# Writing the attention mask of every second token tile into PSUM with ScalarE instead of two products on TensorE

## The reference

```
qkv = x @ Wqkv;  q, k, v = split(qkv)            # 16 heads of 64
q = rope(l2norm(q) * qs);  k = rope(l2norm(k) * ksc)
sim = einsum('bhwie,bhwje->bhwij', q, look(k)) * 8      # 32 queries x 64 keys a window
mask = (it < jb) | (it > jb + w) | (jb == -1)
sim = where(mask, -big, sim);  attn = softmax(sim)
out = einsum('bhwij,bhwje->bhwie', attn, look(v)) @ Wo
x = out + x
x = (a * gelu(gate)) @ W2 + b2 + x                # a, gate from layernorm(x) @ W1
```

## Time and profile before

| what | value |
|---|---|
| median of 3 runs | 4778.22 us |
| lowest and highest | 4775.92 and 4784.65 us |
| the profiled execution's own time | 4772.76 us |
| span of the profile | 4771.0 us |
| mean granted clock of PE | 0.958 |
| transformer stage in the span | about 200 to 3600 us |
| busy over the span | PE 91%, DVE 66%, ACT 57%, POOL 55% |

### The profile page before, as it was taken

One profiled execution on the slowest core, in us unless ns is written; L12 is line 12 of the kernel. 1 busy time (PEld: TensorE's weight loads), 2 busy tenths in 40 slices (PEclk: granted clock), 3 DMA queues, 4 the chain that ended last, 5 costly groups with the idle time before them and its releaser, 6 DMA issues. The chain is left out here.

```text
span 4771.0 us, 155839 instructions
## 1 busy us (share of the span) xinstructions
PE 4331.5 (91%) x69192; PEld 2789.7 (58%) x69192; DVE 3143.9 (66%) x4110; ACT 2702.9 (57%) x3930; POOL 2624.7 (55%) x1468
## 2 busy tenths in 40 slices
PE   7489999999999999999999999999974999788878
PEld 5256666666666666666666666666652554344435
DVE  3467776767677766777776766777733443599975
ACT  4246666656666666566656665666642343577743
POOL 0266666666666666666666666666632222477752
PEclk8689999999999999999999999999986999799989
DMA  2111112211222112211122122222111000211100
GB/s 56 52 33 42 47 45 63 49 47 43 51 57 52 44 44 57 55 46 42 48 65 50 41 48 54 54 49 48 43 34 33 1 1 1 89 75 72 72 35 16
DMA packets 230429, 221.10 MB, mean 46 GB/s; under 512 B 137656, under 2 KB 185793, under 8 KB 227713
## 3 DMA queue, kind: packets, MB, share of 16 engines
q1 hardware_dynamic: 229761, 211.13, 16.9%
HBM read 68.50 MB, written 4.03 MB: 15 GB/s over the span
## 5 line engine op out<-in xcount | busy, mean ns | idle before, releaser
L1018 POOL TENSOR_TENSOR tf_qk<-tf_qk,tf_rot 128x1024 f32<-128x1024 f32 x384 | 908.3, 2365 | 1099.5 <-DVE tf_rot L1392 1099.5
L1025 POOL TENSOR_TENSOR tf_qk<-tf_qk,tf_rn 128x1024 f32<-128x1024 f32 x384 | 722.3, 1902 | 126.2 <-ACT tf_rn L1273 125.5
L1084 PE MATMUL tf_psum<-tf_Wqkv,tf_xsT 128*128 128x512 f32 x1536 | 737.6, 603 | 41.5 <-issue 20.6
L1266 ACT ACTIVATE tf_sq<-tf_psum 128x1024 f32<-128x1024 f32 x384 | 393.1, 1024 | 502.8 <-DVE tf_rot L1392 502.8
L1388 DVE TENSOR_TENSOR tf_qk<-tf_psum,tf_table 128x1024 f32<-128x1024 f32 x384 | 467.4, 1217 | 219.4 <-PE tf_psum L1084 218.4
L1398 DVE TENSOR_REDUCE tf_ss<-tf_sq 128x16 f32<-128x1024 f32 x384 | 457.6, 1192 | 23.5 <-ACT tf_sq L1266 23.5
L1392 DVE TENSOR_TENSOR tf_rot<-tf_psum,tf_table 128x1024 f32<-128x1024 f32 x384 | 466.2, 1214 | 0.0
L1084 PEld LDWEIGHTS tf_psum<-tf_Wqkv,tf_xsT 128*128 128x128 f32 x1536 | 271.2, 192 | 320.6 <-issue 294.1
L1066 PE MATMUL tf_psum<-ident,tf_qk 128*128 128x128 f32 x3072 | 416.4, 279 | 7.3 <-issue 4.9
L1149 PE MATMUL tf_psum<-tf_probT,tf_Vback 64*64 64x32 f32 x12288 | 383.3, 221 | 29.8 <-DVE tf_z L1433 15.6
L1066 PEld LDWEIGHTS tf_psum<-ident,tf_qk 128*128 128x128 f32 x3072 | 349.1, 143 | 95.4 <-issue 87.5
(11 more groups left out here) (319 smaller groups left out, 7960.9 us busy)
## 6 DMA issues: line engine op xcount, KB each, us to landing
tf_Vback<-tf_V SPq DMA_DIRECT2D x384, 128.0 KB
tf_Vback<-tf_V SPq DMA_DIRECT2D x576, 64.0 KB
mb_Csb<-mb_kept SPq DMA_DIRECT2D x16, 2048.0 KB, 7.1
tf_zr<-z SPq DMA_DIRECT2D x96, 128.0 KB, 2.7
z<-tf_z SPq DMA_DIRECT2D x48, 256.0 KB, 2.5
tf_Wqkv<-in_Wqkv_split SPq DMA_DIRECT2D x18, 512.0 KB, 3.7
tf_zu<-z SPq DMA_DIRECT2D x97, 64.0 KB
tf_zu<-z SPq DMA_DIRECT2D x97, 63.5 KB
```

Of the source, the lines that this page charges most:

```text
L1018: nc.gpsimd.tensor_tensor(v, v, rot[:, kind, :], ALU.add).then_inc(added.sem, 1)
L1025: nc.gpsimd.tensor_tensor(v, v, rn[:, t, HEADS * kind:HEADS * (kind + 1)].unsqueeze(2) .to_broadcast([P, HEADS, HD]), ALU.mult).then_inc(n ...
L1084: last = nc.tensor.matmul(proj[:, half, :], xsT[:, step.unit(0), WIN + t * P:WIN + (t + 1) * P], Wqkv[:, c:c + 512], start=True, stop=True)
L1266: nc.scalar.activation(sq[:, kind, :], flat2(proj), ACT.Square).then_inc(squared.sem, 1)
```

## The change

For odd tiles (the second of a unit, `t` = 1) the two mask products are left out, and PE waits for a new event `opened` instead of `v_kept`. ACT writes the mask: `open_scores`, one ACTIVATE with the function Copy from the f32 mask in SBUF (`mask32`, the same 64 columns repeated for 16 heads) into both `score` banks, 128x1024. It stands in ACT's queue right behind `keep_v` in every even step (for the tile whose scores follow in the next, odd step), and waits for `keep_v` by its own semaphore `v_kept`. Even tiles keep their two products. No DMA and no other engine's instruction is changed.

```diff
@@ scores(step) on PE
                 pe.wait_ge(copied, place(step.before(), "k") + 2)
-                pe.wait_ge(v_kept.sem, v_kept.at(tau - 1, 1))
-                for odd in range(2):
-                    nc.tensor.matmul(score[:, odd, :], identb[:, :], mask[:, t:t + 1, :].to_broadcast([P, PAIRS, HD]),
-                                     start=True, stop=False, skip_group_check=True)
+                if t:
+                    pe.wait_ge(opened.sem, opened.at(tau // 2, 1))
+                else:
+                    pe.wait_ge(v_kept.sem, v_kept.at(tau - 1, 1))
+                    for odd in range(2):
+                        nc.tensor.matmul(score[:, odd, :], identb[:, :], mask[:, t:t + 1, :].to_broadcast([P, PAIRS, HD]),
+                                         start=True, stop=False, skip_group_check=True)
@@ on ACT
+            def open_scores(step):
+
+                act.wait_ge(v_kept.sem, v_kept.at(step.tile(2), 1))
+                nc.scalar.activation(score.rearrange("p b (a e) -> p (b a) e", e=HD),
+                                     mask32[:, 1:2, :].to_broadcast([P, HEADS, HD]), ACT.Copy).then_inc(opened.sem, 1)
@@ body(step) on ACT
                 if step.has(2):
                     keep_v(step)
+                    if step.k % 2 == 0:
+                        open_scores(step)
                 if step.has_input():
```

More of the change, by code:

```diff
@@ L844, in transformer_stage @@
         v_done, v_kept, pv_done, laid = ev("v_done"), ev("v_kept"), ev("pv_done"), [ev("laid0", 64), ev("laid1", 96)]
-        scored, maxed, centred, exped, den_sum, den_inv, prob_ready, o_copied, out_done, z_added = (
-            ev(n) for n in "scored maxed centred exped den_sum den_inv prob_ready o_copied out_done z_added".split())
+        scored, opened, maxed, centred, exped, den_sum, den_inv, prob_ready, o_copied, out_done, z_added = (
+            ev(n) for n in "scored opened maxed centred exped den_sum den_inv prob_ready o_copied out_done z_added".split())
         ln_stats, ln_moments, ln_logged, ln_rstd, xn_centred, xn_ready = (
@@ L1253, in _ @@
         def _(act):
-            for e in (squared, logged, rn_ready, v_kept, exped, o_copied, ln_logged, ln_rstd, gelued):
+            for e in (squared, logged, rn_ready, v_kept, opened, exped, o_copied, ln_logged, ln_rstd, gelued):
                 e.start(act)
```

## The result

The changed kernel takes 4842.73 us (median of 4 runs, 4839.4 to 4862.6) against 4779.9 us for the kernel before in the same session: a ratio of 1.0143, 95% interval 1.0124 to 1.0162. By the medians that is slower by 63 us, by the ratio by 68 (59 to 77), where the sum said 46. Measured again in a later session it was 1.0151 (1.0135 to 1.0167).

The account below looks back on a forecast made before the run. It took an ACT and DVE path to bound about 15 of some 66 us, PE the other 51. Terms +49.2, -4.7 and +1.5 at the edges gave +46.0, so 4824 us, likeliest range 4815 to 4833, 8 in 10 4798 to 4848.

Parts of the forecast that it names:

- The path over ACT and DVE without slack in step 3: From the kT copy in step 2 to `attend` in step 3: 15.12 us without slack, bounding the kernel there.
- the slot of 0.52 us on PE: PE's time for an odd tile's mask products before its scores; 96 x 0.52 = 49.9 us removed from PE's queue.
- step 2 to step 3: 46 places where the new ACT operation delays `gelu 1` and `attend` by 1.07 us, PE's saving lost: +49.2 us.
- step 0 to step 1: 47 places where scores wait for ACT's mask, so only 0.10 of the 0.52 us is won: -4.7 us.
- the argument against the clock: Each new wait is under 1 us, and the stage holds clock 0.99 with waits up to 0.5 us every period.
- The rival's price of 69 us: Longer waits lower PE's clock, `output` taking 1.49 us more in each of 46 periods: 69 us more, 4893; chance 0.05.
- The likeliest case's own range: Whole kernel, 4815 to 4833 us: bounds of the sum and the 5 us by which medians may differ; chance 0.82.
- the wider range: Whole kernel, 8 in 10: 4798 to 4848 us, for absorbed delays below and part of the clock's price above.
- the large term: The 46 step 2 to step 3 places at 1.07 us each: +49.2 us.
- theory D1: From the experiments: stalls sit at fixed places of PE's stream; removing four records per odd tile exposed them, 15 to 20 us.
- The faster rival: PE is the bound everywhere, all 96 slots are won and ACT's work hides in idle time: 4728 us; chance 0.07.
- The rival of a short operation: New ACT operation takes only 0.5 us, so step 2 costs +24.4 and step 1 wins -24.4: 4778 us; chance 0.06.

Follow-up runs that it names:

- step 1 only: Against the kernel before, mask from ACT only for the 48 tiles of step 0 to step 1; step 3 tiles keep their products: 1.0046, +22 us.
- step 1 only, stand-ins: Against the kernel before, mask from ACT in step 0 to step 1 only, plus two one-column products behind the wait for it: 1.0055, +26 us.
- wait only: Kernel before with all products; in step 0 ACT also copies into a spare SBUF tile, and PE waits for it in step 1: 1.0077, +37 us.
- the run without products: Kernel before without the mask products of odd tiles and nothing in their place: 0.9989, -5 us.

## Why the prediction was right and where it was wrong

**Right: what bounds the kernel.** The path over ACT and DVE without slack in step 3, and PE outside of it. Lengthened by ACT's operation alone it cost 54 us (49.2 worked out), shortened on ACT it gave 8; the slot of 0.52 us on PE, taken out alone, went into a longer wait of `attend` there. One reading of the rows was a little too strong: the 44 waits of the earlier trace rows hold two outside of the 46 periods, so PE waited for `add_output` in 42 of them; in the other four the distance is the same, 15.12 to 15.19 us.

**Right: step 2 to step 3.** The distance grew by 1.06 us (1.07 worked out), with the waits where they were placed, 0.50 for the square (0.6), though in some 32 periods only, and 0.69 for `add_output` (0.8). The price of the new operation, 1.03 us, lay within its bounds of 1.01 to 1.06.

**Wrong: step 0 to step 1.** The step that failed is "Of the 0.52 us only 0.10 are won: 47 x 0.10 = -4.7", with "this is PE's to keep". The period without a stall did win its 0.09 to 0.10. But the place as a whole costs +22 us, measured alone. The sum put two things at nothing. The first is what PE has in hand when its own stream stops: before the change its last wait was free 1.3 us before the scores, with the change 0.14 us, and nine times or so in the scores of step 1 a stall then shows in greater part. The second is the clock behind these longer stalls. The table gives the stretches from the scores of step 1 to the next scores, 46 of them, in sum against the first profile of the kernel before. Of that, stalls (of any PE group) and the time of PE's operations make up the whole; the last column is how long the granted clock was 0.5.

| kernel | longer by, us | stalls | operations | clock at 0.5, us |
|---|---|---|---|---|
| before, first and second profile | 0, 1.9 | 0, 0.4 | 0, 1.4 | 0, 3.4 |
| step 1 only | 24.7 | 8.0 | 16.6 | 34.1 |
| step 1 only, stand-ins | 24.6 | 9.8 | 14.8 | 30.7 |
| changed kernel, first and second profile | 15.7, 22.9 | 6.8, 10.6 | 8.8, 12.3 | 13.7, 23.9 |
| wait only | 9.5 | 6.3 | 3.1 | 3.4 |

So some 7 to 11 us of the failed step are stalls and 9 to 17 are PE's operations at its low level: half of the time at 0.5 is lost, and 34.1 and 23.9 us give 17 and 12. 54 + 22 = 76 us for the two parts measured apart, where the whole change measured 68 and 72.

**Wrong in part: the argument against the clock.** "Each new wait is under 1 us, where that one was 6.68" looked at the waits that the change makes and not at those that are there and get longer. Behind a stall of 2.2 us the transposes took 1.97 us instead of 1.09. The rival's price of 69 us did not come: in step 3 the clock was at 0.5 for 75 us in the first profile of the changed kernel and for 27 in the second, against 41 and 48 before. But a price that the sum had at nothing came in step 1. It doesn't follow from the length of the stall alone: in the kernel with the change in step 1 only, a stall of 2.76 us left the clock high.

**The range and the sign.** The likeliest case's own range, 4815 to 4833, was missed: 4842.7 lies above it, 19 us above the 4824, and the 20 or so us that were missing are the failed step. That the wider range, up to 4848, holds the result is luck in part. It had been widened for a part of the clock's price, but in step 3, and not for longer stalls. The sign is right by the large term, for its own reason. The rows for the missing term were in the trace: the list of waits had "L1125 <- issue: 16.2, 15, 1.9". I read it as noise of the stream, since nobody releases it, and took it to be the same in both kernels.

The faster rival, PE as the bound everywhere, is refuted by the run without products: 50 us less work, 5 us less time. The rival of a short operation is refuted by the 1.03 us that the operation takes. The Trainium skill's section "Identifying the Most-Contended Engine" (page "Perfetto Trace Analysis") would, taken by busy time, have led to it; this case's trace does not agree that the engine with the highest busy share is the one to relieve, since PE, busy for 97% of the stage, waited some 0.35 us for another path in 42 of 46 periods. The section itself wants the tensor engine judged by the arithmetic that it does and by its weight loads, not by its busy matmuls, and by the weight loads (PEld, 397 of 600 us, against DVE's 426) PE would not have come first.

**What stays open.** What PE waits for in a stall was not found. It is tied to the instruction and not to the time, it is there with or without the change, and it shows only the part that the time since the last release does not cover. The traces do say where it comes. In the 14 profiles the distance from one stall of over 0.3 us to the next, counted in matmul records of PE, is a multiple of 126.3 (505 = 4 x 126.3, 632 = 5 x, 2653 = 21 x), to within 2 records in 646 of 702 cases. A tile has 333 records before the change, so the stream has two or three such places in every tile, if they go on where nothing is seen, and most are covered. Eight tiles have 2664 records before the change and 2656 after it. With a stall each 2653, the place within the scores moves back by 11 records from one to the next before, and by 3 after, so the stalls fall on other groups of PE, as theory D1 had it. That it is the supply of instructions is a guess. The same page of the Trainium skill ("Tensor Engine Instruction") draws a semaphore wait ahead of the queue that feeds the array, which fits that a late release leaves nothing in hand; no run here looks into that queue. When the clock falls behind a stall and when not is open too, and with it why the missing time of step 1 was 16 us in one profile of the changed kernel and 23 in the other.

## What to carry to other kernels

Look for the path that ends just in front of the busy engine's waits: a wait of 0.35 us that comes in nearly every period says that the work removed from the busy engine is lost there, and the work added to the other is paid in full. And where the busy engine has stalls of its own, a long cheap instruction in front of many short ones is cover for them; before taking it out, or putting a late wait behind it, compare how early the last wait is free with how long behind a release those stalls end (here some 4 us). A change measured in two halves (only the added work, only one of the places) told here in two runs what the whole had mixed.

## What the runs showed of the hardware

- PE stops at fixed places of its stream of instructions, at distances that are multiples of 126.3 matmul records, for up to 2.8 us within the scores; in two profiles of one kernel the tiles are nearly the same, and two added products per odd tile move them. What is seen of a stop shrinks with the lead, from 2.2 to 2.5 us at 0.14 to none at 2.9, and PE goes on 3.4 to 4.7 us behind the release of its last wait.
- Behind a stall of 2.2 us PE ran at its low level, a granted clock of 0.50: 1.97 us for eight transposes of 128x128, 1.09 at the high one; behind 1.54 us at the same instruction it did not.
- An ACTIVATE with Copy, f32, 128x1024 with a repeated source in SBUF, takes 1028 ns into PSUM (mean of 96). The copy of v on DVE, of the same size out of PSUM, took 1.23 us where ACT takes 1.01.
